# A fused attention and feed-forward kernel: two chunks of the output product in three float32r passes, and part of the final normalization on GpSimd

## The reference

```
q      = x @ Wq + bq                        # 16 heads of 32
k      = key_param @ Wk + bk                # 32 patterns; v = k @ Wv + bv
A      = sparsemax(q k^T / sqrt(32))        # per head, over the 32 patterns
x      = layernorm(x + (A v) @ Wo + bo)
s      = x @ Win + bin                      # 64 units
g      = sum_h relu(s * W1[:, h] + b1[:, h]) * W2[:, h] + b2     # 16 h
out    = layernorm(x + g @ Wout + bout)
```

## Time and profile before

| | us |
|---|---|
| median of three runs (1311.59 to 1316.35) | 1313.4 |
| the profiled execution, its own time | 1313.41 |
| its span, first to last instruction | 1311.6 |
| TensorE busy in the span (share) | 1248.0 (95%) |
| VectorE busy | 1133.2 (86%) |
| ScalarE busy | 1068.2 (81%) |
| GpSimd busy | 676.5 (52%) |

### The profile page before, as it was taken

One profiled execution on the slowest core, in us unless ns is written; L12 is line 12 of the kernel. 1 busy time (PEld: TensorE's weight loads), 2 busy tenths in 40 slices (PEclk: granted clock), 3 DMA queues, 4 the chain that ended last, 5 costly groups with the idle time before them and its releaser, 6 DMA issues. The chain is left out here.

```text
span 1311.6 us, 25223 instructions
## 1 busy us (share of the span) xinstructions
PE 1248.0 (95%) x5848; PEld 853.4 (65%) x5848; DVE 1133.2 (86%) x4538; ACT 1068.2 (81%) x2285; POOL 676.5 (52%) x1634
## 2 busy tenths in 40 slices
PE   8973899999999999999999999999999999989995
PEld 5642566676766767676776767677676767655552
DVE  3986899899999999999999999999999999966776
ACT  3661865779898888989898888989898888987776
POOL 1431333346555555655565555656555555665654
PEclk9995999999999999999999999999999999999998
DMA  6480785655656556565656656565655656468874
GB/s 203 131 215 17 199 246 192 191 185 171 218 184 216 198 197 206 190 217 182 220 188 208 203 191 214 185 220 183 213 196 199 211 186 216 162 227 281 280 233 104
DMA packets 92181, 258.35 MB, mean 197 GB/s; under 512 B 16067, under 2 KB 16067, under 8 KB 75622
## 3 DMA queue, kind: packets, MB, share of 16 engines
q1 hardware_dynamic: 91862, 256.26, 60.0%
q10 hardware_dynamic: 144, 0.26, 0.1%
HBM read 206.13 MB, written 50.33 MB: 196 GB/s over the span
## 5 line engine op out<-in xcount | busy, mean ns | idle before, releaser
L856 PE MATMUL bank<-G_sb,pT 128*128 128x512 f32 x1024 | 462.5, 594 | 2.8 <-DMA G_sb<-G_of_heads 2.1
L856 PEld LDWEIGHTS bank<-G_sb,pT 128*128 128x128 f32 x1024 | 185.2, 191 | 188.6 <-issue 184.3
L1426 DVE SCALAR_TENSOR_TENSOR acc<-hinge,w2c,acc 128x512 f32<-128x512 f32 x210 | 157.1, 748 | 81.7 <-ACT hinge L1019 80.2
L541 POOL TENSOR_TENSOR shift_sq<-sum,per_row_sq 128x1 f32<-128x1 f32 x244 | 95.2, 390 | 252.4 <-DVE y_sb L1269 250.5
L1376 DVE MAX8 top<-bank 128x8 f32<-128x32 f32 x2048 | 211.8, 178 | 0.0
L749 PE MATMUL bank<-A_hi,xT_hi 128*128 128x512 f32 x512 | 203.3, 397 | 0.0
L751 PE MATMUL bank<-A_hi,xT_lo 128*128 128x512 f32 x512 | 202.7, 396 | 0.0
L750 PE MATMUL bank<-A_lo,xT_hi 128*128 128x512 f32 x512 | 202.6, 396 | 0.0
L1019 ACT ACTIVATE hinge<-s_sb,b1c,w1c 128x512 f32<-128x512 f32 x240 | 192.8, 806 | 0.0
L1075 ACT CAST xT_hi<-bank 128x512 fp32r<-128x512 f32 x127 | 74.1, 584 | 134.8 <-PE bank L751 134.8
L989 ACT ACTIVATE unread<-y_sb,shift_sq 128x512 bf16<-128x512 f32 x244 | 174.5, 715 | 7.7 <-POOL minus_mean L543 7.5
(11 more groups left out here) (164 smaller groups left out, 2461.7 us busy)
## 6 DMA issues: line engine op xcount, KB each, us to landing
G_sb<-G_of_heads SPq DMA_DIRECT2D x128, 1024.0 KB, 5.5
x_sb<-in_L_attn_query_dram SPq DMA_DIRECT2D x128, 256.0 KB, 4.7
y_sb<-in_L_attn_query_dram SPq DMA_DIRECT2D x256, 128.0 KB, 5.4
out_dram<-o_sb SPq DMA_DIRECT2D x230, 128.0 KB, 4.7
G_of_heads<-y_sb SPq DMA_DIRECT2D x64, 256.0 KB, 4.0
out_dram<-y_sb SPq DMA_DIRECT2D x11, 256.0 KB, 3.3
y_sb<-in_L_attn_Wk_dram SPq DMA_DIRECT2D x1, 1024.0 KB, 5.9
y_sb<-in_L_attn_Wq_dram SPq DMA_DIRECT2D x1, 1024.0 KB, 8.1
```

The source lines that it names most:

```text
L541: nc.gpsimd.tensor_tensor(shift_sq[:, par:par + 1], total[:, par:par + 1], per_row_sq[:], ALU.mult).then_inc(s_mean, 1)
L856: mm = nc.tensor.matmul(o_ps[i % 2][:], pT[:, bass.ds(pair_place(turn, i) + (i % H * C + c) * P, P)], G_sb[:, i % GR, c, :], start=(c == 0 ...
L1426: nc.vector.scalar_tensor_tensor(acc[:], hinge[:, k % HR, :], w2c[:, k:k + 1], acc[:], ALU.mult, ALU.add).then_inc(s_acc, 1)
```

## The change

- Probabilities lie in 20 blocks of four heads by one chunk (`SETS` = 5) in place of two turns (8192 columns become 10240); a table `blocks` says where each is. The columns that ScalarE writes at once are now contiguous.
- `G_sb` becomes a ring of three buffers of 6 x 512 columns. `G_of_heads` gets eight groups of columns (`G_COLS`): the four raw chunks and the high and low parts of chunks 1 and 3.
- For tiles 0 to 15 GpSimd makes the parts of chunk 1, for tiles 16 to 31 those of chunk 3, from the G loaded for the product (a rounding copy and a subtraction of 128x512 each), and SP stores them.
- Tiles 16 to 31 take chunk 1 in three float32r passes, tiles 32 to 105 chunks 1 and 3, tiles 106 to 127 none. GpSimd makes the high and low parts of the probabilities of those chunks (128x128 or 128x256, `LAG_PART`), a slot before the product.
- G's load for tiles from 35 on is issued a slot earlier, in slot i+21. It has 1, 1.25 or 1.5 MB.
- From slot 56 to slot 130 the final normalization into `o_sb` is GpSimd's (`pool_finishes`), no longer ScalarE's.
- `mean` makes one column in place of two; the squares are scaled by 1 and `ve` scales by 1/D. Some small tiles lie in others.

```diff
-LAG_G = 22
+LAG_G = 21
+LAG_PART = 22
...
-        GR, STAGES = 2, 2
+        GR, STAGES, SETS = 3, 2, 5
...
-        pT = sb("pT", [P, 2 * H * C * P])
+        pT = sb("pT", [P, SETS * C * HPC * P])
+        part_hi = sb("part_hi", [P, 2, 2 * P], F32R)
+        part_lo = sb("part_lo", [P, 2, 2 * P], F32R)
...
-        G_sb = sb("G_sb", [P, GR, C, D])
+        G_sb = sb("G_sb", [P, GR, 6, D], F32R)
+        G_hi = sb("G_hi", [P, 2, D], F32R)
...
+        def pool_finishes(turn, j):
+
+            return turn * UNROLL + j >= LAG_WO + 2 * UNROLL + 1 and not vector_finishes(turn, j)
...
+        PARTS_MADE = (1, 3)
+        PLAIN_FROM = TILES - 22
+
+        def parts_of(i):
+            chunks = PARTS_MADE[:i // UNROLL] if i < PLAIN_FROM else ()
+            return sorted(chunks, key=lambda c: block_of(i, c))
...
+            LAG_MADE = LAG_WO + 1
+            def G_loads(n):
+                return [i for i, early in ((n - LAG_G - 1, False), (n - LAG_G, True))
+                        if 0 <= i < TILES and early == (i >= len(PARTS_MADE) * H + GR)]
...
+                if in_range(turn, j, LAG_MADE) and made_of(base + j - LAG_MADE) is not None:
+                    i = base + j - LAG_MADE
+                    sp.wait_ge(s_made, i + 1)
+                    store_made(i)
+                for i in G_loads(base + j):
...
+                    if i >= GR:
+                        sp.wait_ge(s_o, i - GR + 1)
+                        if made_of(i - GR) is not None:
+                            sp.wait_ge(s_made_st[i % GR], made_stores(i - GR))
...
GpSimd, mean and norm:
-                nc.gpsimd.tensor_tensor(shift_sq[:, par:par + 1], total[:, par:par + 1], per_row_sq[:],
-                                        ALU.mult).then_inc(s_mean, 1)
...
-                nc.gpsimd.tensor_tensor(ve[:], var[:, par:par + 1], eps[:], ALU.add).then_inc(s_ve, 1)
+                nc.gpsimd.tensor_scalar(ve[:], var[:, par:par + 1], 1.0 / D, EPS, ALU.mult, ALU.add).then_inc(s_ve, 1)
...
GpSimd, slot, after both norms and before both and split:
+                    if pool_finishes(turn, j):
+                        i += base
+                        pool.wait_ge(s_final, i)
+                        pool.wait_ge(s_shift2, i + 1)
+                        pool.wait_ge(s_store[i % OR], 32 * (i // OR))
+                        nc.gpsimd.tensor_scalar(o_sb[:, i % OR, :], y_sb[:, i % YR, :], rstd2[:, i % 2:i % 2 + 1],
+                                                shift2[:, i % 2:i % 2 + 1], ALU.mult, ALU.add).then_inc(s_final, 1)
...
GpSimd, slot, after split and before mean:
+                if in_range(turn, j, LAG_PART) and parts_of(base + j - LAG_PART):
...
+                    pool.wait_ge(s_o, i - 1)
+                    nc.gpsimd.tensor_copy(hi, rows).then_inc(s_phi, 1)
+                    pool.wait_ge(s_phi, parts_before(i) + 1)
+                    nc.gpsimd.tensor_tensor(lo, rows, hi.bitcast(F32), ALU.subtract).then_inc(s_plo, 1)
+                if in_range(turn, j, LAG_WO) and made_of(base + j - LAG_WO) is not None:
...
+                    nc.gpsimd.tensor_copy(made_hi(i), G_of(i, made_of(i), "raw").bitcast(F32)).then_inc(s_made_hi, 1)
...
GpSimd, slot, last, after the folds:
+                    nc.gpsimd.tensor_tensor(made_lo(i), G_of(i, made_of(i), "raw").bitcast(F32),
+                                            made_hi(i).bitcast(F32), ALU.subtract).then_inc(s_made, 1)
...
TensorE:
+            def output_product(i):
+                o, plain, in_parts = o_ps[i % 2], plain_of(i), parts_of(i)
+                for c in plain:
+                    mm = nc.tensor.matmul(o[:], p_blocks[:, block_of(i, c), i % HPC, :], G_of(i, c, "raw").bitcast(F32),
+                                          start=(c == plain[0]), stop=(not in_parts and c == plain[-1]))
+                if in_parts:
+                    pe.wait_ge(s_plo, parts_before(i) + 1)
+                for n, c in enumerate(in_parts):
+                    hi, lo = (part[:, i % 2, n * P:(n + 1) * P] for part in (part_hi, part_lo))
+                    nc.tensor.matmul(o[:], hi, G_of(i, c, "hi"), start=False, stop=False)
+                    nc.tensor.matmul(o[:], hi, G_of(i, c, "lo"), start=False, stop=False)
+                    mm = nc.tensor.matmul(o[:], lo, G_of(i, c, "hi"), start=False, stop=(c == in_parts[-1]))
+                return mm
...
-                    for c in range(C):
-                        mm = nc.tensor.matmul(o_ps[i % 2][:],
-                                              pT[:, bass.ds(pair_place(turn, i) + (i % H * C + c) * P, P)],
-                                              G_sb[:, i % GR, c, :], start=(c == 0), stop=(c == C - 1))
-                    mm.then_inc(s_o, 1)
+                    output_product(base + i).then_inc(s_o, 1)
...
ScalarE:
-                if in_range(turn, j, LAG_FINAL) and not vector_finishes(turn, j):
+                if in_range(turn, j, LAG_FINAL) and not vector_finishes(turn, j) and not pool_finishes(turn, j):
```

More of the change, by code:

```diff
@@ L163, in build_kernel @@
         second = sb("second", [P, GROUP * P], F32R)
+        ones_row = second[0:1, 0:P].bitcast(F32)
         bin_sb = sb("bin_sb", [P, 1])
@@ L221, in build_kernel @@
         s_vT, s_vTc, s_Gmm, s_Gev = sem("s_vT"), sem("s_vTc"), sem("s_Gmm"), sem("s_Gev")
+        s_made_hi, s_made = sem("s_made_hi"), sem("s_made")
+        s_made_st = [sem(f"s_made_st{r}") for r in range(GR)]
+        s_phi, s_plo = sem("s_phi"), sem("s_plo")
         s_Gst = [sem(f"s_Gst{r}") for r in range(STAGES)]
@@ L353, in so_far, with block_of, plain_of, parts_before @@
             return min(max(n, 0), TILES) if isinstance(n, int) else n
-        def pair_place(turn, i):
-            return (turn + i // UNROLL) % 2 * (H * C * P)
+        blocks, spare = [{(n, c): n * C + c for n in range(C) for c in range(C)}], list(range(C * C, C * C + C))
+        for _ in range(1, TILES // UNROLL):
+            old = blocks[-1]
+            blocks.append({(n, c): old[c - 1, n] if c else spare[n] for n in range(C) for c in range(C)})
+            spare = [old[C - 1, c] for c in range(C)]
+        p_blocks = pT[:].rearrange("p (b a n) -> p b a n", a=HPC, n=P)
+        def block_of(i, c):
+            return blocks[i // UNROLL][i % H // HPC, c]
+        PARTS_MADE = (1, 3)
[3 more added lines that the diff above has]
+            return sorted(chunks, key=lambda c: block_of(i, c))
+        def plain_of(i):
+            return [c for c in range(C) if c not in parts_of(i)]
+        def parts_before(i):
+            return sum(bool(parts_of(n)) for n in range(i))
+        def made_of(i):
+            return PARTS_MADE[i // UNROLL] if i // UNROLL < len(PARTS_MADE) else None
+        MADE_HI, MADE_LO = 4, 5
+        def made_hi(i):
+            return G_sb[:, i % GR, MADE_HI, :] if i < H else G_hi[:, i % 2, :]
+        def made_lo(i):
+            return G_sb[:, i % GR, MADE_LO, :]
+        def made_stores(i):
+            return sum(16 if n < H else 32 for n in range(i % GR, i + 1, GR))
+        def G_cols(i):
+            wanted = [G_COLS.index((c, "raw")) for c in plain_of(i)]
+            wanted += [G_COLS.index((c, part)) for c in parts_of(i) for part in ("hi", "lo")]
+            assert max(wanted) - min(wanted) + 1 == len(wanted)
+            return min(wanted), max(wanted) + 1
+        def G_of(i, c, kind):
+            return G_sb[:, i % GR, G_COLS.index((c, kind)) - G_cols(i)[0], :]
+        def parts_rows(i):
+            places = [block_of(i, c) for c in parts_of(i)]
+            if len(places) == 1:
+                return slice(places[0], places[0] + 1)
+            return slice(places[0], places[1] + 1, places[1] - places[0])
         def turns_of(turn, j, lag, ring):
@@ L534, in _, with mean @@
             pool.wait_ge(s_const, CONSTS)
-            def mean(t0, par, s_rows, total, s_mean, minus_mean, shift_sq, s_shift):
+            def mean(t0, par, s_rows, total, s_mean, minus_mean, s_shift):
                 if not isinstance(t0, int) or t0 >= 3:
@@ L618, in slot @@
                     fold(s_above, base + i + 1, above, s_folds)
+                if in_range(turn, j, LAG_WO) and made_of(base + j - LAG_WO) is not None:
+                    i = base + j - LAG_WO
+                    pool.wait_ge(s_made_hi, i + 1)
+                    nc.gpsimd.tensor_tensor(made_lo(i), G_of(i, made_of(i), "raw").bitcast(F32),
+                                            made_hi(i).bitcast(F32), ALU.subtract).then_inc(s_made, 1)
             slots(pool, slot)
```

117 lines of the change are left out of this document (59 added, 58 removed).

## The result

The changed kernel takes 1299.37 us (median of four runs, 1299.09 to 1299.62) against 1313.2 us of the kernel before: ratio 0.9892, 95% interval 0.9873 to 0.9910. It is faster by 13.8 us; 1291 us had been forecast, with a range of 1281 to 1304. The profiled execution took 1299.16 us, its span is 1297.4.

What follows compares the result with a forecast made beforehand. TensorE was taken to set the 9.20 us slot, with VectorE close behind. From the profiled 1313.41 us, -21.5 (two-chunk tiles) + 2.2 (G's parts' stage) - 3 (end) = -22.3 gave 1291 us, range 1281 to 1304.

Steps and rivals of the forecast that it cites:

- The passes: TensorE's products: a chunk in three float32r passes takes 0.6975 us in place of 0.860, 26.65 us saved in all.
- I take 0: Inside one TensorE product: the step from float32 into float32r costs nothing; bounds 0 and 7 us.
- the wait for `s_plo`: TensorE, mid-product: costed at nothing, as GpSimd fills the ring a slot earlier; without that cover about 1.1 us.
- What GpSimd's work does to VectorE: From slot 56: large GpSimd operations hold back VectorE's SBUF operations, an extra stall between 0 and 1.9 us a slot.
- E: VectorE's extra stall a slot from GpSimd's new work: 0.27 us, slot 8.91, 21.5 us gained over 74 tiles.
- The 8.64 us: VectorE alone, before any extra stall: 8.47 us busy plus 0.17 of short hand-overs a slot.
- Two of the signs: VectorE, if the forecast is right: hinge wait shrinks from 0.56 to nearly nothing, `twice` lengthens from its mean of 0.30.
- GpSimd's sum: GpSimd from slot 56: new work less two `shift_sq` columns adds 1.9 us to 5.25, no bound by itself.
- G's parts' stage: Slots 23 to 54: VectorE at 9.31 us in slots 35 to 54, +2.2 us; upper bound +24 us.
- The end: After the last scores: earlier issue and third buffer remove seven waits for G's load, -3 us, bounds 0 and 3.4.
- (a): Rival: TensorE stays the only bound, nothing lost in the parts' stage; 1284 us, chance 0.20.
- (e): Rival: loads of G become the bound, needing a landing of more than two slots; chance within the rest.

Runs made afterwards that it cites:

- `act_final`: Changed kernel with the final normalization back on ScalarE in all slots up to 130; 1297.30 us (one run).
- `pool_early`: Changed kernel with the final normalization on GpSimd from slot 40 in place of 56; 1294.31 us (one run).
- `g_late`: Changed kernel with every load of G issued in slot i+22 as before the change, ring of three kept; 1297.65 us (one run).
- `no_make`: Changed kernel without GpSimd's rounding copy and subtraction for G's parts, SP storing raw columns of the same size; 1284.62 us (one run).
- `pool_double`: Changed kernel with GpSimd doing the 128x512 normalization a second time from slot 64 to 130; 1320.17 us (one run).
- `lo_first`: Changed kernel with GpSimd's subtraction for G's parts moved from its slot's end to right behind the rounding copy; 1291.83 us, ratio 0.9839 to the kernel before.
- `parts_from_32`: Changed kernel with tiles 16 to 31 plain again, no passes before tile 32, G's parts still made; 1291.94 us (one run).

## Why the prediction was right, and where it was wrong

The time fell by 13.8 us, inside the range, 8 us above the forecast. The whole miss is the stage of G's parts. That the two-chunk tiles came out on their number (21.4 us, tiles 32 to 112, where 21.5 were forecast) is luck in part: from tile 40 to 104 a slot gained 0.32 us in place of 0.29, 2 us more, and tiles 32 to 40, still under the end of G's parts, gained 0.6 in place of 2.3.

**The passes** came as forecast: 3.11 us a product (3.12 forecast), 0.32 us a slot, 0.163 for one chunk. "I take 0" for the step into float32r held. So did the wait for `s_plo` at nothing: in the steady stage 1.0 us in all before weight loads, none before matmuls.

**What GpSimd's work does to VectorE** was wrong in sign. The step said "E = 0.27: VectorE 8.91, so the slot becomes 8.91". Measured is 8.88 with TensorE full, VectorE at 8.17 us busy: E is about -0.3. I had counted what the new operations would hold back and not what they would push out of the way, the `split` that used to meet `u_sb`. `act_final` shows it to be the moved normalization: without the move VectorE is busy 8.46 us a slot. The 8.64 us in which VectorE alone could do a slot was a bound that was never touched. Two of the signs named for the forecast did not come: `twice` has a mean of 277 ns in the steady stage and didn't lengthen, and the wait for the hinge at `acc` is still 0.26 us a slot. GpSimd's sum had a slip: 0.76 + 0.4 + 0.73 is 1.9 without the two columns of 0.19 that were to come off, and 1.5 with them. Measured are 7.11 us a slot, 1.9 more than before, so the figure came out for another reason: the three new operations took 2.0, and `rstd`, which had been taken as unchanged, has a mean of 717 ns in place of 606. The Trainium skill's rule of the exclusive lock ("SBUF — State Buffer", "SBUF: two separate sides") agrees with `u_sb`, which reads two SBUF tiles and has its usual 0.69 us or 1.72 behind a whole `split`; what decides is which two operations meet, and a longer queue can part them.

**G's parts' stage** was the term that failed: forecast +2.2 us with the 2.6 us of the passes lost, measured +10.6 between tiles 16 and 32, with 2.1 us more over TensorE's own time from tile 32 to 40. The step was "In slots 35 to 54 I add 0.4 to E: the subtraction comes last in the slot, where the hinge sum [...] is due, and holds it back in part". It looked at the engine with the least idle time and charged the lock. VectorE did stall there, the hinge sum with `acc` at 953 ns against 746, but that did not set the stage, as `pool_early` shows; the loss came by another way: the subtraction stands between the folds and the norms, ScalarE's final normalization waits for the norm's `shift`, and behind it on ScalarE stand `xT_hi`, `yT` and the `side` that the next folds wait for. My text said "ScalarE still normalizes" and went on. It had named `mean` and the folds as queued behind the new work but not the norms of the next slot, behind the last operation of this one. ScalarE's busy share (131.88 of 157.78 us) hid it: an engine at 84% can be in the turn that sets the slot. The bound of +24 us held.

**The end**: forecast -3, measured -3.3; the reason was half right, as the third buffer did all of it (`g_late`).

Of the rivals, (a) was right for the steady stage and the transfers (e) are excluded by `no_make`. (d), the lock turning the gain around, did not come, but a loss stands nearer than I had put it: one more us on GpSimd made the kernel slower than before (`pool_double`), where the waits recorded are ScalarE's for GpSimd. Sum of the parts by the table: -0.1 + 0 + 10.6 - 0.6 - 20.6 - 0.2 - 3.3 = -14.2 us of span. `lo_first` beats both kernels by its ratio, and `parts_from_32` in a single run reached the same time.

## What to carry to other kernels

Before work is put on an engine with idle time, write down the turn that it will stand in: from this operation, through whoever waits for it, back to what it waits for itself, and sum the turn against the slot. Busy shares don't show it, and where in the engine's slot the same work is put decided here over 7 us (`lo_first`). The sum doesn't tell what two such moves give together: here they didn't add. Whether a load has to be issued earlier or needs another buffer can be told apart with one edit; here the buffer was enough.

## What the runs showed of the hardware that was not expected

VectorE's idle time with no cause that the profile shows ("issue") grew with the change. From the waits of the kernel before, whole span, and of the changed one:

```profile
DVE cum L1393 <- issue: 1.5, 1, 1.5
```

```profile
DVE cum L1516 <- issue: 10.5, 6, 2.5
DVE acc L1549 <- issue: 1.3, 2, 0.9
```

The program's instructions come by DMA queues of their own (0.80 and 1.05 MB), and the traffic beside them rose from 197 to 245 GB/s; all kernels with the larger loads show 7 to 12 us of such stalls at these two lines, single ones of up to 3.4 us. That the traffic delays the instructions is an inference and was not tested. In the steady stage these stalls are hidden, as TensorE is busy for all but 0.4 us. In the stage of G's parts the changed kernel has 2.1 us of them; what they cost there is not shown, and `no_make` hides one of 2.9 us.

The start of the span up to the first product took 182.9 to 184.4 us in different executions, without a relation to the edits, which is up to 1.5 us of uncertainty in every single run above.
